# Key stack loads moved ahead of the first mixture; slot numbers three groups ahead instead of two; one-hots made in their own group; shared products read from PSUM

## The chip, the cores and the metric

One core of a Trainium2 chip runs the whole program. The metric is the device time of one launch in microseconds, the median of three runs: 361.41 us before the change (360.48 to 363.17). One more run was profiled; it took 359.17 us, of which 357.1 us are the span that the trace covers. TensorE is called PE here, VectorE DVE, ScalarE ACT, GpSimd POOL and SyncE SP.

## The reference

Two layers work on x (4 x 256 tokens of 128 features, 1,024 tokens in all) and a context of 96 features. Each layer is a cross attention and then a mixture of experts. The change lies in the first layer's mixture, which is this (E = 64 experts, K = 6 per token, at most CAP = 64 tokens per expert, hidden width 88):

```python
scores = softmax(xf @ gate_w.T)
_, idx = top_k(scores + gate_b, K)
weights = take_along_axis(scores, idx, axis=1)
# tokens of one expert get the positions 0, 1, ... in order; position >= 64 is dropped
xb[expert, pos] = xf[token]
h  = silu(xb @ w1) * (xb @ w3)
yb = h @ w2
y  = zeros.at[token].add(yb[expert, pos] * weight)
z  = silu(xf @ ws1.T) * (xf @ ws3.T) @ ws2.T     # the shared expert, width 176
return y + z
```

The second layer's attention (16 heads of 8 features) follows. It needs its keys in a stacked form, `ks`, which is made of three bf16 parts of the keys. The second mixture (8 experts, 2 per token, width 512) comes last.

## The kernel before

Every engine has its own instruction list, written out by hand; counting semaphores order them, and an engine stops at its first unmet wait. The first mixture works through the 64 experts in 8 groups of 8 (`GE`, `NG`); a group has 8 x 64 = 512 slots, held as 4 pairs of experts with 128 slots each (`NPAIR`). For one group g the steps are:

- `dispatch(g)` (DVE, L1388) compares each token's rank with the slot indices and writes a bf16 0/1 matrix of 4,096 columns into `pbuf`; there are two such buffers.
- `slot_numbers(g)` (PE, L941) multiplies it by the scores and token numbers: 32 matmuls of 10 columns into bank 2.
- `slot_values(g)` (DVE, L1402) reads bank 2 into a slot's weight `wslot`, its token number `token_f` and the integer `slot_token`. Before, these have three buffers.
- Gather (POOL, L507): four indirect DMAs fetch 128 rows of 512 B each from `normalised` in DRAM into `xg`, which has two buffers; gather g waits until `gathered_transposes(g-2)` has read its buffer.
- `gathered_transposes(g)` (PE, L916; transposes at L921) and a copy by ACT (`gathered`, L647) turn the rows into `ctxT`.
- `hidden(g)` (PE, L953), Silu (ACT, L672), product (DVE, L1451), `hidden_transposes(g)` (PE, L966), copy `gT` (ACT, L677), `outputs(g)` (PE): the expert network. The end of `outputs(g)` raises `e_Y`.
- `yh` (ACT, L683) and `yl` (DVE, L1463) split the output in two fp32r parts.
- `slot_onehots(g)` (DVE, L1415; three of the four pairs) and `last_onehot(g)` (ACT, L653; the fourth pair) compare the token numbers with all 1,024 tokens. There are two buffers, in `splits` and in `frbuf`.
- `combine(g)` (PE, L924): 16 matmuls of 512 columns add the group's outputs to their tokens. It runs in the next group, behind `hidden(g+1)` and `slot_numbers`.

The DRAM copy of the normalised rows is stored by ACT (L577), in two halves. SP loads the group weights into a ring of three (`group_weights`, L328; 704 KB and 352 KB); the load for g waits for the outputs of g-3. Behind each of the loads for groups 3 to 6, SP issues two `keys_stacked(i)` (L360), eight in all. Each moves 256 KB from the DRAM scratch `k_parts` to eight partitions of `ks`, one contiguous 32 KB run per partition; rows 8i to 8i+7 for load i. `ks` is first read by the second attention, at 172.1 us in the profile. Everything that SP issues goes through one DMA queue (q1 in the profile); the gathers of POOL go through q0.

The shared expert is computed beside this: `shared_hidden(i)` (PE, L878; two matmuls of 88 x 512 into two banks), `shared_activation(i)` (ACT, Silu of the one and copy of the other), `shared_product(i)` (DVE), for i = 0 to 3, and `shared_outputs` (PE) in group 0, behind `hidden(0)` and `slot_numbers(2)`. `mm` at L772 is the helper through which all matmuls go.

## Time and profile before

| | |
|---|---|
| median of 3 runs | 361.41 us (360.48 to 363.17) |
| profiled execution | 359.17 us, span 357.1 us |
| PE busy | 295.2 us, 83% of the span |
| DVE, ACT, POOL busy | 245.0, 193.0, 139.0 us |
| first mixture, group 0's gather issue to the last `outputs` | 55.2 to 153.1 us |
| share of the chain that ended last | PE 54%, DVE 16%, DMA 11%, of which the gathers 8% |
| DMA | 23.96 MB, 67 GB/s over the span; 130 to 178 GB/s between 80 and 143 us |

Times in the trace count from the start of the span. A window row gives the length of a stretch, the busy time of each engine in it with the number of its instructions, then the granted TensorE clock (1.00 is 2.4 GHz, 0.50 is 1.2 GHz), the mean busy share of the 16 DMA engines and their rate. A DMA packet is counted whole where it starts, so that a long packet shows as a share above 1.00 and then as an empty stretch. In the table of waits a row says how long an engine stood idle before a line, and what ended it. In a row of the timeline the bracket gives the idle time before the instruction and what ended it.

### The profile page before, as it was taken

To read this page: it belongs to the slowest core of one execution; us is meant where nothing else is said; L and a number is where in the kernel's file an instruction comes from. 1 tells how busy PE (TensorE), PEld (TensorE's weight loads), DVE (VectorE), ACT (ScalarE), POOL (GpSimd) and SP (SyncE) were. 2 spreads that over 40 slices of the span, in tenths; PEclk is the share of its full clock that TensorE was granted. 3 is DMA by queue.
4 is the path that set the end of the run, shared out by engine and by line. 5 is a ranking of instruction groups with operands and counts; after the bars stand their busy time and mean duration, and the time that the engine had idled before them with its cause. 6 is when DMAs were issued, how large, how long until landed. Compare 5 with 4: busy or idle time off the path is not lost.

```text
span 357.1 us, 5713 instructions
## 1 busy us (share of the span) xinstructions
PE 295.2 (83%) x2004; PEld 197.3 (55%) x2004; DVE 245.0 (69%) x578; ACT 193.0 (54%) x355; POOL 139.0 (39%) x148
## 2 busy tenths in 40 slices
PE   1996871599777597875489999999898999999995
PEld 0675531458665486662125455554566777777773
DVE  3567799256744523546697787763879988898877
ACT  1355160314344034423227776876696888888881
POOL 5963557464635629274044201010104543254000
PEclk9998795559998879998558999999999999999998
DMA  7923101636899787103405100030000301000001
GB/s 214 281 66 118 30 0 24 38 25 157 155 129 178 162 157 178 61 0 77 87 23 124 23 4 1 3 122 1 0 2 0 105 15 59 0 3 0 0 2 60
DMA packets 12377, 23.96 MB, mean 67 GB/s; under 512 B 2020, under 2 KB 7036, under 8 KB 12029
## 3 DMA queue, kind: packets, MB, share of 16 engines
q1 hardware_dynamic: 10043, 20.39, 22.8%
q0 software_dynamic: 1024, 2.10, 5.8%
q10 hardware_dynamic: 1282, 1.12, 1.1%
q8 instruction: 16, 0.26, 0.3%
q14 instruction: 12, 0.10, 0.1%
HBM read 20.88 MB, written 2.62 MB: 66 GB/s over the span
## 4 chain that ended last, share of the span: by engine, by line
PE 54%; DVE 16%; DMA 11%; ACT 7%; POOL 6%; issue 5%; ACTq 0%; SPq 0%; DVEq 0%; POOLq 0%
PE bank L772 50%; DMA xg<-normalised,slot_token 8%; POOL xg L507 4%; DVE score L1604 2%; DMA packc<-in_packc 2%; DMA big<-q_parts 1%; POOL big L517 1%; DVE pbuf L1393 1%; ACT xnT L658 1%; PE bank L921 1%; DVE xn L1271 1%; POOL rstd L458 1%; PE bank L1102 1%; ACT frbuf L762 1%; ACT pbuf L766 1%
## 5 line engine op out<-in xcount | busy, mean ns | idle before, releaser
L772 PE MATMUL bank<-frbuf,splits 128*128 128x512 f32 x384 | 95.6, 399 | 1.3 <-DVE frbuf L1650 1.0
L772 PEld LDWEIGHTS bank<-frbuf,splits 128*128 128x128 f32 x384 | 69.7, 188 | 21.3 <-issue 5.3
L1650 DVE TENSOR_TENSOR frbuf<-pbuf,frbuf 128x512 fp32r<-128x512 f32 x64 | 53.0, 837 | 11.3 <-ACT pbuf L766 10.5
L507 POOL DMA_INDIRECT xg<-normalised,slot_token x32 | 43.5, 1358 | 41.4 <-DVE slot_token L1413 33.8
L1604 DVE TENSOR_REDUCE score<-bank 128x2 f32<-128x512 f32 x64 | 42.1, 687 | 14.6 <-PE bank L772 13.8
L762 ACT ACTIVATE frbuf<-bank,biases 128x512 fp32r<-128x512 f32 x64 | 44.2, 691 | 13.0 <-PE bank L772 9.6
L738 ACT ACTIVATE pbuf<-bank 128x512 f32<-128x512 f32 x64 | 37.1, 598 | 15.9 <-PE bank L772 15.6
L766 ACT ACTIVATE pbuf<-bank,biases 128x512 f32<-128x512 f32 x64 | 43.8, 684 | 0.0
L772 PE MATMUL bank<-ks,big 128*128 128x256 bf16 x128 | 29.4, 322 | 6.5 <-DVE score L1604 3.7
L552 POOL CAST splits<-ew 128x512 fp32r<-128x512 f32 x16 | 12.7, 796 | 45.6 <-PE bank L772 45.6
L1463 DVE TENSOR_TENSOR frbuf<-bank,frbuf 128x512 fp32r<-128x512 f32 x8 | 5.5, 692 | 33.2 <-ACT frbuf L683 33.2
L677 ACT COPY gT<-bank 88x512 f32<-88x512 f32 x8 | 4.7, 582 | 39.4 <-PE bank L969 39.4
L772 PE MATMUL bank<-big,ks 128*128 128x256 bf16 x128 | 25.2, 285 | 0.4 <-ACT pbuf L738 0.4
L458 POOL TENSOR_TENSOR rstd<-veps,mhalf 128x4 f32<-128x4 f32 (+1 forms) x10 | 9.4, 941 | 37.8 <-DVE veps L1263 35.5
L772 PEld LDWEIGHTS bank<-ks,big 128*128 128x128 bf16 x128 | 9.9, 105 | 25.4 <-DVE score L1604 13.6
L553 POOL TENSOR_TENSOR splits<-ew,splits 128x512 fp32r<-128x512 f32 x16 | 22.3, 1391 | 1.3
L921 PE MATMUL bank<-ident,xg 128*128 128x128 f32 x32 | 6.4, 336 | 18.9 <-DMA xg<-normalised,slot_token 18.9
L772 PE MATMUL bank<-pbuf,vaug 128*9 128x256 f32 x256 | 19.7, 381 | 0.0
L537 POOL CAST nmp<-score 128x16 bf16<-128x16 f32 x8 | 1.6, 198 | 44.5 <-DVE score L1604 44.5
L1393 DVE TENSOR_TENSOR pbuf<-rk,iota_s 128x4096 bf16<-128x4096 bf16 (+1 forms) x10 | 18.5, 1863 | 0.1
L772 PE MATMUL bank<-frbuf 128*128 128x512 f32 (+1 forms) x80 | 16.7, 357 | 1.9 <-ACT frbuf L683 1.9
L651 ACT COPY ctxT<-bank 128x512 f32<-128x512 f32 x8 | 4.7, 585 | 24.5 <-PE bank L921 24.5
(195 smaller groups left out, 529.5 us busy)
## 6 DMA issues: line engine op xcount, KB each, us to landing
big<-in_w SPq DMA_DIRECT2D x8, 704.0 KB
ew<-in_ew SPq DMA_DIRECT2D x16, 256.0 KB, 3.1
big<-in_w SPq DMA_DIRECT2D x8, 352.0 KB
ks<-k_parts SPq DMA_DIRECT2D x8, 256.0 KB
big<-q_parts SPq DMA_DIRECT2D x8, 192.0 KB
k_parts<-parts SPq DMA_DIRECT2D x1, 768.0 KB, 3.9
x<-in_x SPq DMA_DIRECT2D x2, 256.0 KB, 5.5
normalised<-xn ACTq DMA_DIRECT2D x2, 256.0 KB, 2.3
```

The costliest lines, as they stand in the source:

```text
L458: pool.tensor_tensor(out=rstd[:, cs], in0=veps[:, cs], in1=mhalf[:, 0:n], op=ALU.pow).then_inc(ln_rstd, 1)
L507: pool.indirect_dma_start(out=xg[:, g % 2, j, :], out_offset=None, in_=xn_dram, in_offset=bass.IndirectOffsetOnAxis(ap=slot_token[:, g % 3 ...
L552: chained(pool.tensor_copy(high[:, e % 2, :], ew[:, e % RING1, i, :]))
L553: pool.tensor_tensor(out=low[:, e % 2, :], in0=ew[:, e % RING1, i, :], in1=high[:, e % 2, :].bitcast(F32), op=ALU.subtract).then_inc(split, 1)
L738: a.activation(prob1[:, e % NPROB, :], bank[2 + e % 2][:, :], ACT.Exp).then_inc(a_exp, 1)
L762: a.activation(acth[:, n % NA, :], bank[n % 3][:, :], ACT.Gelu, bias=bias).then_inc(f_hi, 1)
L766: a.activation(act[:, n % 4, :], bank[n % 3][:, :], ACT.Gelu, bias=bias).then_inc(f_act, 1)
L772: return pe.matmul(out_, lhsT, rhs, start=start, stop=stop, skip_group_check=True)
L921: ins = pe.transpose(bank[3][:, chunk(j)], xg[:, g % 2, j, :], ident[:, :])
L1393: v.tensor_tensor(out=view(onehots[g % 2][:, c * GS:c * GS + 1], (CAP0, n * GE), (2, CAP0 // 2), (1, 2)), in0=view(rk[:, g, c, 0, 0:1], (2 ...
L1604: v.tensor_reduce(nm1[:, c, 2 * hp:2 * hp + 2], bank[m % 2][:, :].rearrange("p (h k) -> p h k", h=2), X, ALU.max, negate=True).then_inc(a_ ...
L1650: v.tensor_tensor(out=actl[:, n % NA, :], in0=act[:, n % 4, :], in1=acth[:, n % NA, :].bitcast(F32), op=ALU.subtract).then_inc(f_lo, 1)
```

## The change

The change has four parts. SP issues all eight `keys_stacked` loads in one go, as soon as the normalised rows are stored (`xn_out` is 32) and before the loads of groups 3 to 7. PE computes `slot_numbers` three groups ahead, with `wslot`, `token_f` and `slot_token` in four buffers. The one-hots of group g are made in group g itself, on DVE behind the product of group g and on ACT behind its Silu, no longer one group earlier. The shared product reads its second factor from PSUM, so ACT's copies go away; in exchange `shared_hidden(2)` and `(3)` wait for DVE's products 0 and 1, and PE now runs them behind `slot_numbers(0)`.

The diff, without hunks in which only `g % 3` becomes `g % NS`:

```diff
--- before.py
+++ after.py
@@ -181,9 +181,10 @@
 
         xb = ctxT[:, :].rearrange("p (a s) -> p a s", a=2)
         PTs = [splits[:, :, :], frbuf[:, 1024:1024 + NPAIR * T].rearrange("p (j t) -> p j t", j=NPAIR)]
-        wslot = sb("wslot", [P, 3, NPAIR])
-        slot_token = sb("slot_token", [P, 3, NPAIR], U32)
-        token_f = sb("token_f", [P, 3, NPAIR])
+        NS = 4
+        wslot = sb("wslot", [P, NS, NPAIR])
+        slot_token = sb("slot_token", [P, NS, NPAIR], U32)
+        token_f = sb("token_f", [P, NS, NPAIR])
         token_i = sb("token_i", [P, NC, 2], I32)
         xg = sb("xg", [P, 2, NPAIR, P])
         sil, gv = sb("sil", [P, NPAIR, I0]), sb("gv", [P, NPAIR, I0])
...
@@ -362,13 +363,14 @@
                              kscratch[PARTS_K[i]].rearrange("(d h) t -> d h t", d=HD)
                              ).then_inc(ks_in, 16)
 
+            sp.wait_ge(xn_out, 32)
+            for i in range(NCOMB):
+                keys_stacked(i)
+
             for g in range(RING0, NG):
 
                 sp.wait_ge(e_Y, g - RING0 + 1)
                 group_weights(g)
-                if g < RING0 + NCOMB // 2:
-                    keys_stacked(2 * (g - RING0))
-                    keys_stacked(2 * (g - RING0) + 1)
 
             sp.wait_ge(sh_sb, 4)
             for e in range(2):
...
@@ -625,9 +627,8 @@
                     norm_transposed(2)
             def shared_activation(i):
                 a.wait_ge(sh_ps, i + 1)
-                a.activation(shared_silu(i), bank[SH_BANKS[i][0]][0:I0, :], ACT.Silu)
-                a.copy(hs[i // 2][:, half(i % 2)], bank[SH_BANKS[i][1]][0:I0, :]
-                       ).then_inc(sh_sil, 1)
+                a.activation(shared_silu(i), bank[SH_BANKS[i][0]][0:I0, :], ACT.Silu
+                             ).then_inc(sh_sil, 1)
 
             a.wait_ge(c_all, 1)
             a.copy(vaug[:, :, :, HD:HD + 1],
...
@@ -663,7 +664,6 @@
 
             gathered(0)
             a.wait_ge(c_iota, 1)
-            last_onehot(0)
             for g in range(NG):
                 for p2 in range(2):
                     a.wait_ge(e_H, 2 * g + p2 + 1)
...
@@ -673,12 +673,12 @@
                                  bank[5 + p2][:, 0:2 * SI].rearrange(
                                      "p (j i) -> p j i", j=2)[:, :, 0:I0],
                                  ACT.Silu).then_inc(e_sil, 1)
+                last_onehot(g)
                 a.wait_ge(e_gTp, g + 1)
                 a.copy(gT[:, :, :], bank[4][0:I0, :].rearrange(
                     "p (j s) -> p j s", j=NPAIR)).then_inc(e_gT, 1)
                 if g + 1 < NG:
                     gathered(g + 1)
-                    last_onehot(g + 1)
                 a.wait_ge(e_Y, g + 1)
                 a.copy(yh, bank[7][:, :].rearrange("p (j d) -> p j d", j=NPAIR)).then_inc(e_yh, 1)
 
...
@@ -903,11 +903,7 @@
             gate_ranks(0)
             pe.wait_ge(x1_sb, NC)
             shared_hidden(1)
-            pe.wait_ge(sh_sil, 1)
-            shared_hidden(2)
             gate_ranks(1)
-            pe.wait_ge(sh_sil, 2)
-            shared_hidden(3)
 
 
             def onehot(g, c, j):
...
@@ -982,18 +978,21 @@
 
             pe.wait_ge(g_parts, 2)
             slot_numbers(0)
+            for i in (2, 3):
+                pe.wait_ge(sh_sb, i - 1)
+                shared_hidden(i)
             slot_numbers(1)
-            pe.wait_ge(sh_sil, 4)
             gathered_transposes(0)
+            slot_numbers(2)
+            pe.wait_ge(sh_sb, 4)
             for g in range(NG):
                 hidden(g)
-                if g + 2 < NG:
-                    slot_numbers(g + 2)
+                if g + 3 < NG:
+                    slot_numbers(g + 3)
                 if g >= 1:
                     combine(g - 1)
                 else:
                     pe.wait_ge(ld_small, 64)
-                    pe.wait_ge(sh_sb, 4)
                     shared_outputs(0)
                     shared_outputs(1)
                 hidden_transposes(g)
...
@@ -1404,13 +1403,13 @@
                 v.wait_ge(e_W, g + 1)
                 for s in range(2):
                     ps = slice(64 * s, 64 * s + 64)
-                    v.reduce_sum(wslot[ps, g % 3, :],
+                    v.reduce_sum(wslot[ps, g % NS, :],
                                  view(bank[2][ps, NW * s:NW * s + 1], (2 * NW, NPAIR), (1, 3)), X)
                     ins = v.reduce_sum(
-                        token_f[ps, g % 3, :],
+                        token_f[ps, g % NS, :],
                         view(bank[2][ps, NW * s + 3:NW * s + 4], (2 * NW, NPAIR), (1, 2)), X)
                 chained(ins)
-                v.tensor_copy(slot_token[:, g % 3, :], token_f[:, g % 3, :]).then_inc(e_id, 1)
+                v.tensor_copy(slot_token[:, g % NS, :], token_f[:, g % NS, :]).then_inc(e_id, 1)
 
             def slot_onehots(g):
 
...
@@ -1418,28 +1417,27 @@
                 if g >= 2:
                     v.wait_ge(e_comb, g - 1)
                 for j in range(NPAIR - 1):
-                    ins = v.tensor_scalar(PTs[g % 2][:, j, :], iota_t, token_f[:, g % 3, j:j + 1],
+                    ins = v.tensor_scalar(PTs[g % 2][:, j, :], iota_t, token_f[:, g % NS, j:j + 1],
                                           None, ALU.is_equal)
                 ins.then_inc(e_PTv, 1)
 
             def shared_product(i):
 
-                part = hs[i // 2][:, half(i % 2)]
                 v.wait_ge(sh_sil, i + 1)
-                v.tensor_tensor(out=part, in0=part, in1=shared_silu(i),
-                                op=ALU.mult).then_inc(sh_sb, 1)
+                v.tensor_tensor(out=hs[i // 2][:, half(i % 2)], in0=bank[SH_BANKS[i][1]][0:I0, :],
+                                in1=shared_silu(i), op=ALU.mult).then_inc(sh_sb, 1)
 
             dispatch(0, range(4, 8))
             dispatch(1, range(0, 4))
             slot_values(0)
+            for i in range(4):
+                shared_product(i)
             dispatch(1, range(4, 8))
-            shared_product(0)
             slot_values(1)
             dispatch(2)
-            for i in range(1, 4):
-                shared_product(i)
+            slot_values(2)
+            dispatch(3)
             v.wait_ge(c_iota, 1)
-            slot_onehots(0)
             for g in range(NG):
                 v.wait_ge(e_id, g + 1)
 
...
@@ -1449,15 +1447,14 @@
                 for j in range(NPAIR):
                     at = (j % 2) * SI + I0
                     ins = v.scalar_tensor_tensor(out=gv[:, j, :], in0=bank[5 + j // 2][:, at:at + I0],
-                                                 scalar=wslot[:, g % 3, j:j + 1], in1=sil[:, j, :],
+                                                 scalar=wslot[:, g % NS, j:j + 1], in1=sil[:, j, :],
                                                  op0=ALU.mult, op1=ALU.mult)
                 ins.then_inc(e_gv, 1)
-                if g + 2 < NG:
-                    slot_values(g + 2)
                 if g + 3 < NG:
-                    dispatch(g + 3)
-                if g + 1 < NG:
-                    slot_onehots(g + 1)
+                    slot_values(g + 3)
+                slot_onehots(g)
+                if g + 4 < NG:
+                    dispatch(g + 4)
 
                 v.wait_ge(e_yh, g + 1)
                 v.tensor_tensor(out=yl, in0=bank[7][:, :].rearrange("p (j d) -> p j d", j=NPAIR),
```

On PE, ahead of group 0. The rows with `sparts,pbuf` are `slot_numbers` (32 each), those with `xnT,packa 88x512` `shared_hidden` (2 each), `ident,xg` is `gathered_transposes(0)`, `big,ctxT` is `hidden(0)`, and `qbuf,ws` the first of `shared_outputs`. Before:

```order
L772 MATMUL bank<-xnT,packa 88x512 x2
L772 MATMUL bank<-sparts,pbuf 128x10 x64
L921 MATMUL bank<-ident,xg 128x128 x4
L772 MATMUL bank<-big,ctxT 64x176 x8
L772 MATMUL bank<-sparts,pbuf 128x10 x32
L772 MATMUL bank<-qbuf,ws 128x512
```

After the change:

```order
L772 MATMUL bank<-sparts,pbuf 128x10 x32
L772 MATMUL bank<-xnT,packa 88x512 x4
L772 MATMUL bank<-sparts,pbuf 128x10 x32
L917 MATMUL bank<-ident,xg 128x128 x4
L772 MATMUL bank<-sparts,pbuf 128x10 x32
L772 MATMUL bank<-big,ctxT 64x176 x8
L772 MATMUL bank<-sparts,pbuf 128x10 x32
L772 MATMUL bank<-qbuf,ws 128x512
```

`slot_numbers(0)` has moved ahead of two `shared_hidden`, and `slot_numbers(2)` from behind `hidden(0)` to ahead of it.

On SP, from the store of the key parts on. Before:

```order
L357 DMA k_parts<-parts 128x3x1024
L331 DMA big<-in_w 128x1408
L333 DMA big<-in_w 88x1024
L361 DMA ks<-k_parts 8x16384 x2
L331 DMA big<-in_w 128x1408
L333 DMA big<-in_w 88x1024
L361 DMA ks<-k_parts 8x16384 x2
```

After the change:

```order
L358 DMA k_parts<-parts 128x3x1024
L362 DMA ks<-k_parts 8x16384 x8
L332 DMA big<-in_w 128x1408
L334 DMA big<-in_w 88x1024
L332 DMA big<-in_w 128x1408
L334 DMA big<-in_w 88x1024
```

The eight key loads stand together, and the five loads of group weights follow with nothing between them.

On ACT, one group in the middle of the mixture (`ctxT` is the copy of the gathered rows, `xnT` and `frbuf` or `splits` the one-hot, the CAST of `frbuf<-bank` is `yh`). Before:

```order
L677 COPY gT<-bank 88x512
L651 COPY ctxT<-bank 128x512
L658 ACTIVATE xnT<-ew,token_f 128x1024
L661 ACTIVATE frbuf<-xnT 128x1024
L683 CAST frbuf<-bank 128x512
L672 ACTIVATE sil<-bank 128x176 x2
```

After the change:

```order
L672 ACTIVATE sil<-bank 128x176 x2
L659 ACTIVATE xnT<-ew,token_f 128x1024
L662 ACTIVATE frbuf<-xnT 128x1024
L678 COPY gT<-bank 88x512
L652 COPY ctxT<-bank 128x512
L683 CAST frbuf<-bank 128x512
```

The one-hot no longer stands between the copy of the gathered rows and `yh`.

## Rows read from the trace of the kernel before

**Rows 1.** Windows by stage: length, busy PE PEld DVE ACT POOL, clock, DMA, GB/s.
```profile
54.20:65.40 11.20, 1.01 (x32) 0.93 (x32) 8.49 (x15) 0.00 (x0) 8.65 (x6) 0.50 0.19 26
65.40:81.50 16.10, 15.35 (x86) 9.48 (x88) 5.72 (x13) 5.68 (x9) 7.55 (x6) 0.50 0.52 31
81.50:89.50 8.00, 7.76 (x90) 6.49 (x88) 6.33 (x14) 3.34 (x7) 3.94 (x2) 1.00 0.69 171
89.50:101.40 11.90, 8.50 (x92) 6.64 (x90) 6.58 (x15) 4.05 (x8) 8.01 (x7) 1.00 0.87 164
101.40:112.30 10.90, 8.13 (x92) 6.64 (x90) 6.31 (x14) 4.22 (x8) 5.24 (x4) 1.00 0.83 144
112.30:126.60 14.30, 10.58 (x92) 8.49 (x90) 6.42 (x14) 5.09 (x9) 6.20 (x5) 0.74 0.81 152
126.60:136.50 9.90, 9.10 (x92) 7.14 (x90) 4.36 (x13) 3.40 (x7) 4.29 (x5) 0.87 0.97 200
136.50:144.90 8.40, 7.01 (x60) 5.73 (x58) 3.58 (x7) 4.30 (x8) 8.34 (x2) 1.00 0.42 108
144.90:153.10 8.20, 6.63 (x54) 5.14 (x50) 3.23 (x7) 2.99 (x6) 0.47 (x1) 1.00 0.20 66
```
**Rows 2.** Waits of PE, 40 to 155 us: us in total, times, longest.
```profile
PE bank L921 <- DMA xg<-normalised,slot_token: 18.9, 5, 9.0
PE bank L772 <- ACT frbuf L683: 3.1, 4, 1.2
```
**Rows 3.** The chain that ended last, 52 to 160 us: start, us, what.
```profile
60.70 4.64 DMA xg<-normalised,slot_token
...
100.35 10.24 DMA xg<-normalised,slot_token
...
122.74 12.07 DMA xg<-normalised,slot_token
```
**Rows 4.** DMA answer for 86.3 to 86.95 us: packets, MB, share of 16 engines.
```profile
q1 hardware_dynamic: 27, 0.29, 317.2%
```
**Rows 5.** DMA answer for 86.95 to 89.1 us.
```profile
DMA packets 0, 0.00 MB, mean 0 GB/s; under 512 B 0, under 2 KB 0, under 8 KB 0
```
**Rows 6.** DMA answer for 89.75 to 91.8 us.
```profile
q1 hardware_dynamic: 16, 0.26, 101.1%
q0 software_dynamic: 15, 0.03, 22.8%
```
**Rows 7.** DMA answer for 93.25 to 99.3 us, the queue of SP.
```profile
q1 hardware_dynamic: 222, 1.00, 60.8%
```
**Rows 8.** The page's part 6: issues, KB each, us from issue to landing.
```profile
normalised<-xn ACTq DMA_DIRECT2D x2, 256.0 KB, 2.3
```
**Rows 9.** Timeline, stores and loads: start, us, engine, line, operation.
```profile
39.62 0.39 ACTq L577 DMA_DIRECT2D normalised<-xn  x1
...
81.54 0.34 SPq L331 DMA_DIRECT2D big<-in_w  x1
```
**Rows 10.** Window behind the weight load's issue at 81.54 us.
```profile
82.50:82.75 0.25, 0.25 (x8) 0.10 (x5) 0.00 (x0) 0.25 (x2) 0.00 (x0) 1.00 1.79 248
```
**Rows 11.** Timeline, the steps ahead of group 0 and in it.
```profile
37.43 3.44 PE L772 MATMUL bank<-xnT,packa 128*88 128x512 f32 x4
...
54.22 1.22 DVE L1393 TENSOR_TENSOR pbuf<-rk,iota_s 128x2048 bf16<-128x2048 bf16 x1
...
55.35 0.68 DVE L1429 TENSOR_TENSOR qbuf<-qbuf,ew 88x512 f32<-88x512 f32 x1
...
65.47 1.09 PE L921 MATMUL bank<-ident,xg 128*128 128x128 f32 x4 [8.96 <-DMA xg<-normalised,slot_token]
...
67.24 2.62 PE L772 MATMUL bank<-big,ctxT 128*64 128x176 f32 x16 [0.68 <-ACT ctxT L651]
...
69.79 1.02 PE L772 MATMUL bank<-sparts,pbuf 128*128 128x10 bf16 x32
...
71.80 2.29 DVE L1393 TENSOR_TENSOR pbuf<-rk,iota_s 128x4096 bf16<-128x4096 bf16 x1
```

More of the change, by code:

```diff
@@ L509, in _ @@
                         in_offset=bass.IndirectOffsetOnAxis(
-                            ap=slot_token[:, g % 3, j:j + 1], axis=0)).then_inc(e_xg[g], 16)
+                            ap=slot_token[:, g % NS, j:j + 1], axis=0)).then_inc(e_xg[g], 16)
             ones_pair = 0x3F803F80
@@ L657, in last_onehot @@
                     a.wait_ge(e_comb, g - 1)
-                a.activation(xnT[:, :], iota_t, ACT.Abs, bias=token_f[:, g % 3, 3:4], scale=-1.0
+                a.activation(xnT[:, :], iota_t, ACT.Abs, bias=token_f[:, g % NS, 3:4], scale=-1.0
                              ).then_inc(a_step, 1)
```

## The prediction

> **What bounds the kernel now.** I read the windows by stage first [rows 1]. They cut the first mixture at the ends of `outputs(g)`: group 0 ends at 81.5 us, group 7 at 153.1 us. From 81.5 us on PE is the engine with the most work, but only group 1 (81.5 to 89.5) runs without a hole: 8.0 us, PE busy for 7.76. Groups 2 to 5 do the same work and take 11.9, 10.9, 14.3 and 9.9 us. Groups 6 and 7 have no `slot_numbers` left and take 8.4 and 8.2. Ahead of all this PE is nearly idle from 54.2 to 65.4 us, and its granted clock is 0.50, that is 1.2 GHz, until 81.5.
>
> The table of waits names the holes [rows 2]: `gathered_transposes` waits five times for the gather, 18.9 us in all. The longest, 9.0 us, is gather 0, so 9.9 us belong to four later groups. Four more waits, 3.1 us together and at most 1.2, are `combine` waiting for `yh` from ACT. The chain shows how late a gather lands behind its last issue [rows 3]: 4.64 us in group 0, 10.24 and 12.07 us later.
>
> The DMA answers say what those gathers stand behind. Where the two key loads of group 0 begin, 27 packets take 317% of 16 engines for 0.65 us, 33.0 us of packet time [rows 4]; 0.26 of the 0.29 MB are one key load, eight packets of 32 KB. If the 19 small ones took 2.4 us together, a key packet took 3.8. Then no packet at all starts for 2.1 us [rows 5], though gathers have been issued. The second key load is 16 packets (eight are data), 101.1% of 16 engines over 2.05 us, 33.2 us or 4.1 us for each large one [rows 6]. So a key load of 256 KB keeps eight DMA engines for 4 us, and the next follows on the same eight. The next group's weights, 1.00 MB, move only behind it [rows 7]. The key loads are what makes the gathers late.
>
> **The change, part by part.**
>
> *Key loads out of the mixture, and the slot numbers three groups ahead.* Gather g+3 now starts when its buffer comes free, behind `gathered_transposes(g+1)`, at the end of group g. It is needed two groups later, about 16 us; before, it also had to wait for the slot numbers made in the middle of the group, which left a group and a half, some 12 us. With 0.5 MB less per group ahead of it, it should be in time. I take all four waits as gone.
>
> *One-hots in their own group.* ACT's two passes leave the stretch between the copy of the gathered rows and `yh`. They now stand behind Silu, where ACT is idle during `combine` (it is busy 3.3 of 8.0 us [rows 1]); DVE's three are hidden in the same way, as it is busy 6.33 of 8.0. If that cover were gone, the 3.1 us of waits for `yh` would come back.
>
> *The pace after.* Four groups with `slot_numbers` at 8.0 us, three without. For these, 8.4 less 1.2 is 7.2 and 8.2 less the mean wait of 0.8 is 7.4; I take 7.3. That is 32.0 + 21.9 = 53.9 us in the place of 71.6 [rows 1, 2]: a gain of **17.7 us**. It is made of 9.9 of gather waits, 3.1 of waits for `yh`, 1.0 for a `slot_numbers` that moves ahead, and 3.7 mostly for the half clock of groups 4 and 5 (0.74 and 0.87). Next late in this stage is nothing but PE.
>
> *The key loads' new place.* The second half of the rows is stored at 39.62 us and lands 2.3 us later, at 41.9 [rows 8, 9]. A load's first packets start about 1.0 us behind its issue [rows 9, 10], so the train begins near 43.0. SP has nothing else to do until 81.5. But the last issue of gather 0 is at 60.70 us [rows 3], in the middle of the train, and its packets go to the same engines. Eight loads at 3.97 us (the mean of 3.8 and 4.1) are 31.8 us, to 74.8. The lower bound is no hindrance at all. The upper is what the mixture's worst period leaves: 14.3 us less the weights' own 3.7 us (60.8% of 6.05 us [rows 7]), halved, is 5.3 us per load, 42.4 in all. I take the middle, since it is the duration of these very packets with only gathers beside them. The trace speaks for a wait to the end of the train: gather packets issued during the first key load had to let the second go first [rows 5, 6]. One more microsecond, an estimate from the crowding of 1.1 us per gather packet there, and `gathered_transposes(0)` starts at 76, not at 65.47 [rows 11].
>
> The Trainium skill says otherwise (DMA: Bandwidth & Descriptors, "Queues, rings and completion order"): an engine goes round its queues in turn, packet by packet, so each of the four gather packets on it would wait for one key packet only. By that the sum would be some 4 us better, as rival 2 works out.
>
> *Group 0 itself.* From those transposes to the end of `outputs(0)` it was 81.5 - 65.47 = 16.0 us at half clock. `slot_numbers(2)` now stands ahead of `hidden(0)`: transposes 1.09 + 1.02 against a start 1.77 us behind before, 0.4 more. `slot_numbers(3)` then waits for DVE, 0.6 for the values and 2.29 for `dispatch(3)`, instead of following `hidden(0)` after 2.55: 0.5 more [rows 11]. So 16.9 us: group 0 ends at 92.9, **11.4 us later**.
>
> *The shared expert.* The two `shared_hidden` that move behind `slot_numbers(0)` cost 3.44 us each at half clock [rows 11], from 55 (a product of 0.68 us behind 54.22) to 62; then Silu 0.6 and product 0.7, with DVE waiting, then the second half of `dispatch(1)` 1.22, then `slot_numbers(1)` 1.0: PE is ready for the transposes at 65.6. Under a gather that lands at 76 this costs nothing. If the gather is early it is next. The copies that ACT loses (four) lie beside other work: nothing. A product from PSUM I price like one from SBUF, 0.68 us.
>
> *The tail.* POOL clears `big` behind the last `outputs`, as before; its long memset of `ks` follows gather 7 and ends before that. The rest of the program moves as a block.
>
> **Sum.** 17.7 - 11.4 = 6.3 us. The span goes from 357.1 to 350.8 us, the profiled execution from 359.17 to 352.9. The median of the three runs is 2.2 us above the profiled one; I add that: **355.1 us**.
>
> **Rivals.**
>
> 1. *Forecast*, 355.1, its own range 352 to 358 (a key load of 3.5 to 4.3 us). Chance 0.42.
> 2. *Turn by turn.* Gather packets slip in between key packets. The train's gaps lie at 43.0 + 3.97k: 58.9, 62.9, 66.8 and 70.8 us, so the fourth gather packet is through at about 72, and group 0 ends at 88.9: 4 us better than the forecast, 351. For it: nothing forbids it once both queues are deep. Against: [rows 5, 6]. Chance 0.20.
> 3. *No collision* (the loads run faster alone, or gathers pass). Then the shared expert's path decides: transposes at 65.6; `slot_numbers(2)` needs values and `dispatch(2)`, to 68.5, and ends at 69.6; `hidden(0)` starts 2.4 us later than before, plus the 0.5: 17.7 - 2.9 = 14.8, so 346.6. Against: 4 us per load is measured. Chance 0.12.
> 4. *Same within measurement.* The train is as forecast, but gathers in the mixture are still late for half of their 9.9 us, since each still shares its engines with 1 MB of weights: 6.3 - 5.0 = 1.3, so 360. Chance 0.16.
> 5. *Slower.* The train itself stretches, because gathers 0 and 1 take turns in it while it still holds their last packets. Gain and loss are equal where the transposes start at 82.3, that is at 4.8 us per key load. At the upper bound of 5.3 the train ends at 85.4, group 0 at 103.3, and 21.8 - 17.7 = 4.1 us are lost: 365.5. For it: the periods of 11 to 14 us with two such loads in each. Against: 3.8 and 4.1 where they run alone, as for their first 14 us. Chance 0.10. The Trainium skill (SBUF — State Buffer, "Door 1: The DMA port swizzle") counts eight neighbouring partitions as 2 of 16 ports, which by its 436 GB/s is an estimate of 4.8 us per load; the measured 4.0 is used.
>
> **Chances and range.** A median of three runs here cannot tell less than 1%, 3.6 us, from no change. Faster by more than that: rivals 2 and 3 and nearly all of the forecast, 0.68, with a small part of it taken off for steps that I do not see. Within 1%: 0.20. Slower: 0.12. The range of 347 to 361.5 us leaves out the slow rival, the upper edge of the fourth and a part of the third.
>
> **What would show it.** *The train*: the key loads' packets from 43 us on, the DMA share below full but without end until about 75. *The collision*: `gathered_transposes(0)` waiting for its gather to 76 us; a start near 66 with no such wait is rival 3. *The shared expert*: PE busy between 55 and 62 us at clock 0.50. *The pace*: windows of 8.0 and 7.3 us behind group 0, clock 1.00, no wait of L917 for a DMA, no wait of `combine` for `yh`. A wait there of some microseconds is rival 4. The prediction is wrong if group 0 ends before 87 or after 98 us, or if the seven groups behind it take more than 57 us.

## The result

The changed kernel takes **367.01 us** (median of 4 runs, 366.04 to 369.78), the kernel before 360.95 us in the same session; the ratio is 1.018 (95% interval 1.009 to 1.027). It is slower, by 0.9 to 2.7%; 355.1 us and "faster" were forecast. The profiled execution took 366.04 us against 359.17 before, and the forecast's own sum said 352.9 for it: 13.1 us too little. Executions of one and the same kernel differ here mostly by up to 3%, so every ratio compares fast executions only, while the profiled execution of ones_early, behind_gather0 and padded_onehots_first was a slow one.

### The profile page after: what moved, and what is told of

It is laid out like the page before. It is cut to its first block, busy times and chain, and to the rows that moved or that the text cites. A ratio compares the mean times of both kernels' runs of the same rounds, so it can differ in the third digit from the quotient of the medians.

```text
span 364.0 us, 5706 instructions
## 1 busy us (share of the span) xinstructions
PE 296.2 (81%) x2004; PEld 197.4 (54%) x2004; DVE 250.4 (69%) x578; ACT 192.5 (53%) x351; POOL 133.3 (37%) x148
## 4 chain that ended last, share of the span: by engine, by line
PE 59%; DVE 17%; DMA 9%; ACT 6%; issue 4%; POOL 3%; another core or an unknown queue 1%; ACTq 0%; SPq 0%; DVEq 0%; POOLq 0%
PE bank L772 55%; DMA xg<-normalised,slot_token 6%; DVE frbuf L1420 2%; DVE score L1601 2%; DVE pbuf L1392 2%; DMA packc<-in_packc 2%; DMA big<-q_parts 1%; POOL big L519 1%; POOL xg L509 1%; PE bank L965 1%; ACT gT L678 1%; POOL rstd L460 1%; PE bank L801 1%; PE bank L1101 1%
## 5 line engine op out<-in xcount | busy, mean ns | idle before, releaser
L1647 DVE TENSOR_TENSOR frbuf<-pbuf,frbuf 128x512 fp32r<-128x512 f32 x64 | 52.5, 830 | 11.9 <-ACT pbuf L766 11.5
L509 POOL DMA_INDIRECT xg<-normalised,slot_token x32 | 37.3, 1167 | 48.4 <-DVE slot_token L1412 20.9
L554 POOL CAST splits<-ew 128x512 fp32r<-128x512 f32 x16 | 13.1, 820 | 45.8 <-PE bank L772 45.8
L555 POOL TENSOR_TENSOR splits<-ew,splits 128x512 fp32r<-128x512 f32 x16 | 21.9, 1371 | 1.3
L772 PE MATMUL bank<-frbuf 128*128 128x512 f32 (+1 forms) x80 | 18.0, 378 | 4.8 <-DVE frbuf L1420 4.0
L772 PE MATMUL bank<-xnT,packa 128*88 128x512 f32 (+2 forms) x28 | 17.3, 750 | 3.0 <-DVE qbuf L1427 1.5
L1406 DVE TENSOR_REDUCE wslot<-bank 64x4 f32<-64x12 f32 x16 | 2.7, 168 | 23.7 <-PE bank L772 17.5
L917 PE MATMUL bank<-ident,xg 128*128 128x128 f32 x32 | 5.8, 312 | 15.8 <-DMA xg<-normalised,slot_token 15.8
L772 PEld LDWEIGHTS bank<-frbuf 128*128 128x128 f32 x80 | 14.0, 203 | 7.6 <-DVE frbuf L1420 4.3
```

Of the source, the lines that this page charges most:

```text
L509: pool.indirect_dma_start(out=xg[:, g % 2, j, :], out_offset=None, in_=xn_dram, in_offset=bass.IndirectOffsetOnAxis(ap=slot_token[:, g % N ...
L554: chained(pool.tensor_copy(high[:, e % 2, :], ew[:, e % RING1, i, :]))
L555: pool.tensor_tensor(out=low[:, e % 2, :], in0=ew[:, e % RING1, i, :], in1=high[:, e % 2, :].bitcast(F32), op=ALU.subtract).then_inc(split, 1)
L772: return pe.matmul(out_, lhsT, rhs, start=start, stop=stop, skip_group_check=True)
L1647: v.tensor_tensor(out=actl[:, n % NA, :], in0=act[:, n % 4, :], in1=acth[:, n % NA, :].bitcast(F32), op=ALU.subtract).then_inc(f_lo, 1)
```

## The profile after

The windows by stage, cut where each group's `outputs` ends (length, busy PE, PEld, DVE, ACT, POOL, clock, DMA share, GB/s), answer to [rows 1]. The first stretch is the wait for gather 0, then come groups 0 to 7:

```profile
55.30:80.80 25.50, 6.43 (x40) 2.60 (x40) 6.64 (x11) 1.19 (x2) 9.65 (x8) 0.63 0.60 68
80.80:97.40 16.60, 16.09 (x118) 10.46 (x120) 8.74 (x19) 4.48 (x7) 6.60 (x5) 0.50 0.25 18
97.40:107.20 9.80, 8.39 (x92) 6.45 (x90) 6.49 (x14) 4.38 (x7) 3.37 (x4) 1.00 0.66 138
107.20:115.30 8.10, 7.87 (x92) 6.60 (x90) 4.13 (x13) 4.39 (x7) 4.19 (x5) 1.00 0.86 166
115.30:124.60 9.30, 7.86 (x92) 6.55 (x89) 8.35 (x16) 4.27 (x7) 5.31 (x5) 1.00 0.64 148
124.60:132.70 8.10, 7.87 (x94) 6.63 (x92) 4.74 (x14) 4.39 (x7) 4.69 (x5) 1.00 0.83 168
132.70:139.90 7.20, 6.96 (x58) 5.73 (x56) 5.18 (x8) 4.39 (x7) 6.25 (x5) 1.00 0.77 158
139.90:152.80 12.90, 8.64 (x60) 6.92 (x58) 8.81 (x9) 4.38 (x7) 6.88 (x2) 0.87 0.38 98
152.80:160.10 7.30, 6.63 (x54) 5.10 (x48) 3.64 (x8) 3.91 (x6) 0.00 (x0) 1.00 0.20 67
```

Group 0 ends at 97.4 us where it ended at 81.5, and the seven groups behind it take 62.7 us where they took 71.6. So 15.9 us are lost ahead of group 1 and 8.9 won behind it: 7.0 of the span's 6.9 (364.0 - 357.1). What follows group 7 takes 204 us in both.

The main waits of PE, 40 to 170 us (us in total, times, longest), answer to [rows 2]:

```profile
PE bank L917 <- DMA xg<-normalised,slot_token: 15.8, 1, 15.8
PE bank L772 <- DVE pbuf L1392: 6.6, 4, 2.5
PE bank L772 <- DVE frbuf L1420: 4.0, 1, 4.0
...
PE bank L772 <- ACT frbuf L683: 0.8, 1, 0.8
```

Of the five waits for a gather one is left. It lasts 15.8 us, where the longest was 9.0 and all five together 18.9. The waits for `yh` (L683) went from 3.1 to 0.8. Those for `dispatch` (`pbuf`) grew from 2.6 to 6.6 us; 1.2 of that lie behind group 0. New is one of 4.0 us for DVE's one-hots (L1420). The chain answers to [rows 3], and the first row of the transposes to 65.47 in [rows 11]:

```profile
60.20 20.61 DMA xg<-normalised,slot_token
...
80.86 1.11 PE bank L917 x4
```

The DMA answers (packets, MB, share of 16 engines) answer to [rows 5, 6]. First 50.45 to 59.30 us, where the train is nearly alone; then 62.9 to 68.1, with all four gathers issued:

```profile
q1 hardware_dynamic: 31, 0.52, 50.7%
q0 software_dynamic: 16, 0.03, 1.9%
...
DMA packets 16, 0.26 MB, mean 50 GB/s; under 512 B 8, under 2 KB 8, under 8 KB 8
q1 hardware_dynamic: 16, 0.26, 43.1%
```

Sixteen large packets filled 0.507 x 16 x 8.85 = 71.8 us of engine time, **4.49 us** for each. In the second stretch only key packets start, and no packet of a gather for 5.2 us.

Last, the timeline around group 6 (start, us, engine, line, operation):

```profile
136.28 8.82 DVE L1420 TENSOR_SCALAR frbuf<-ew,token_f 128x1024 fp32r<-128x1024 f32 x3
...
137.19 7.37 POOL L514 MEMSET ks<- 3x8192 int32 x1
...
137.61 7.49 DVE L1420 TENSOR_SCALAR frbuf<-ew,token_f 128x1024 fp32r<-128x1024 f32 x1
...
145.16 2.07 PE L772 MATMUL bank<-frbuf 128*128 128x512 f32 x4 [4.03 <-DVE frbuf L1420]
```

The row at 137.61 is the last of DVE's three one-hots alone. It starts 0.4 us behind POOL's memset and ends at 145.10, 0.5 us behind the memset's end; undisturbed, three take 2.07 us together (ones_early). PE then works at half clock: 0.53, 0.50 and 0.50 in the three microseconds from 145 us, after it had stood idle since 141.1.

## The experiments

Each is told with the profiled execution's two measures: where group 0 ends, and what the seven groups behind it take (after the change 97.4 and 62.7). Where a letter is given, it is the theory or rival of the expectation above it. Behind group 7 come 204 to 206 us in all but keys_late.

### Undo or do the key loads alone

```diff
-            sp.wait_ge(xn_out, 32)
-            for i in range(NCOMB):
-                keys_stacked(i)
 ...
                 group_weights(g)
+                if g < RING0 + NCOMB // 2:
+                    keys_stacked(2 * (g - RING0))
+                    keys_stacked(2 * (g - RING0) + 1)
```

> The changed kernel with one part undone: the eight key loads are sent behind the weights of groups 3 to 6 again, two at a time, as before the change. Theory A: in the changed kernel the early train of key loads is what costs, because gather 0 stands under it until 80.9 us; without it gathered_transposes(0) starts near 66.5 us (65.47 before, plus the 1 us by which slot_values(0) is later), group 0 ends near 82.5, and the seven groups behind it take 57 to 63 us because the gathers, three groups ahead, can stand under a pair of key loads without being waited for. Last group ends near 142 to 145, time 350 to 354 us. Rival B: the pair of key loads sent behind a group still holds the gather that is needed next, and the seven groups take 70 us as before: time about 360. Rival C: the train is harmless and the loss sits in the three-ahead order itself: group 0 ends at 82.5 but the seven groups take more than 75 us: 366.

Measured: 366.16 us, 1.008 times before (1.004 to 1.013). Group 0 ends at 83.7, as theory A said, but the seven groups take 72.8, as rival B said, though not for its reason. The waits of the engines from 83 to 145 us have no wait of PE for a gather among them:

```profile
PE bank L771 <- issue: 11.9, 15, 3.8
...
PE bank L771 <- ACT gT L677: 1.2, 5, 0.2
...
DVE wslot L1405 <- remote: 1.1, 1, 1.1
```

PE stands 11.9 us in pieces for nothing that the profile shows, and its clock was 0.86 in group 1 and 0.75 in group 5. The expectation of 350 to 354 failed: the key loads' new place is not alone at fault.

The counterpart is the kernel before with the early key loads alone (the same lines, the other way round).

> The kernel before with one part of the change alone: the eight key loads are sent right behind the stored rows, all else is as before. Theory A: the train holds gather 0, gathered_transposes(0) starts near 80 us and group 0 ends near 96 us (14.5 us later than before); the waits for gathers in the groups behind are gone, those for yh stay, so the seven groups take about 71.6 - 17 = 55 to 60 us. Sum: -12 to -16 + 14.5, time 358 to 363 us, no difference that can be measured. Rival B: with only two groups ahead the gather of group 1 stands under the train as well and is waited for again behind group 0: 366 us or more. Rival C: the train shortens nothing behind it (the gathers there were slow for another reason): the seven groups still take 70 us, time 374.

Measured: 367.24 us, ratio 1.013 (1.005 to 1.021). Group 0 ends at 93.8, the seven take 67.3; waits for a gather in them fall from 9.9 to 3.9 us. Theory A's mechanism stands, its pace of 55 to 60 us was at least 7 us too good. This part alone makes the kernel slower; the interval overlaps that of the whole change.

### The memset of the ones

```diff
+                if g == 0:
+                    chained(pool.memset(ks[KROWS:KROWS + 3, :, :].bitcast(I32), ones_pair))
 ...
-            chained(pool.memset(ks[KROWS:KROWS + 3, :, :].bitcast(I32), ones_pair))
```

> The changed kernel with the memset of the three rows of ones in the key stack moved from behind the last gather of group 7 (there it runs 137.2 to 144.6 us) to behind the four gathers of group 0 (it would run from about 60 to 68 us, while VectorE waits for the first gather anyway). Theory A: GpSimd's memset holds VectorE's one-hots of group 5 for its whole length (8.82 us for three instructions that take 2.1), and PE waits 4.03 us for them and then runs 3.4 us at half clock: group 6 falls from 12.9 to 7.3 us, time 366.5 - 5.6 = 361 us. Rival B: the one-hots of group 5 are slow for another reason, or the stretch behind only moves the wait to another place: 365 to 367 us. Rival C: the memset now delays slot_values(1), the gathers of group 1 and what hangs on them, and 3 us or more are given back: 364.

Measured: 358.46 us, ratio 0.979 (0.972 to 0.986); its profiled execution took 360.45. Group 6 in windows, with the columns as above:

```profile
139.60:146.90 7.30, 7.07 (x60) 5.78 (x58) 3.64 (x8) 4.41 (x8) 1.81 (x1) 1.00 0.55 142
```

The seven groups take 57.4. The 5.6 us between 12.9 and 7.3 are the memset: the wait of 4.0 us is gone, and so is the half clock behind it. Over the seven groups it is 62.7 - 57.4 = 5.3, as expected. This kernel is the base of those that follow.

### Where the key loads stand, and what makes them slow

```diff
+            sp.wait_ge(e_xg[NG - 1], 16 * NPAIR)
+            for i in range(NCOMB):
+                keys_stacked(i)
             sp.wait_ge(sh_sb, 4)
```

> The kernel ones_early with the eight key loads moved to behind the last gather (SyncE waits for gather 7 to land, then sends all eight, ahead of the expert weights of the second mixture). No key load stands under any gather. Theory A: gathered_transposes(0) starts near 66, group 0 ends near 83, the seven groups behind take the 57.4 us that they took in ones_early or a little less, so the last group ends near 140; behind it come the same 204.2 us as in ones_early, keys_alone and keys_back: span 344 to 346, time 347 us. The keys would land near 155, ahead of the 167 at which the second attention can start. Rival B: the keys now land after the attention wants them, or the expert weights behind them come late: the stretch behind the last group grows by 5 us or more, 352 or above. Rival C: the seven groups are slow whenever gathers and weights run together (keys_back took 72.7 with no wait for a gather), and 5 us or more come back: 352 to 357.

Measured: 365.99 us, ratio 1.008 (1.004 to 1.013). Rival B. The mixture came near what theory A said: transposes(0) at 65.5, group 7 ends at 143.8 and not at 140, which is still 10 us earlier than in ones_early. But PE then waits, 130 to 220 us:

```profile
PE bank L773 <- DMA big<-q_parts: 17.8, 1, 17.8
```

The loads were issued at 131.6, when gather 7 had landed, and the store and loads of the second attention's queries queued behind it. The train costs what stands behind it, wherever that is.

Next, other partitions:

```diff
-                sp.dma_start(ks[i * HD:(i + 1) * HD, :, :],
+                sp.dma_start(ks[i:i + 8 * HD:8, :, :],
```

> The kernel ones_early with the eight early key loads written to other partitions: load i goes to partitions i, i+8, ..., i+56 and not to 8i to 8i+7 (the key stack's rows are then in the wrong order; everything else is computed as before). Same bytes, same eight pieces of 32 KB, same place. Theory A (the way into eight neighbouring partitions sets the 4.5 us of a piece): the pieces fall to 2.0 to 3 us, the train ends near 60 to 65 us in place of 78.3, gather 0 lands near 62 to 67, transposes(0) near 66 to 68 in place of 80.45: span 345. Rival B (the engine's own pace sets it): pieces stay at 4.4 to 4.5 us, gather at 80, span 358. Rival C: a part of both, pieces near 3.5.

This kernel leaves the key stack's rows in another order. Measured: one run, 346.91 us, span 344.8; transposes(0) at 64.99 after a wait of 0.8, against 80.45 in ones_early. The DMA answer for 47.1 to 52.2 us:

```profile
q1 hardware_dynamic: 32, 0.52, 50.2%
```

0.502 x 16 x 5.1 = 41.0 us for sixteen large packets: **2.56 us** each in place of 4.49. The same bytes in the same pieces, on an equal number of engines, differ only in the partitions that they are written to. Theory A.

Then the size of the pieces:

```diff
-        kscratch = nc.dram_tensor("k_parts", [3, P, T], BF16, kind="Internal").ap()
+        kscratch = nc.dram_tensor("k_parts", [3, P, T + 32], BF16, kind="Internal").ap()[:, :, 0:T]
```

> The kernel ones_early with 32 elements of padding behind each 2 KB row of the key scratch in DRAM, and nothing else changed: a load's source is then 128 rows of 2 KB that don't join, so the pieces are 2 KB and not 32 KB. Same place, same bytes, same eight partitions. Theory A (the gather's packets take turns with the key loads piece by piece, and the wait is the size of a piece): gather 0 passes between 2 KB pieces and lands within 3 to 8 us of its issue, though the train itself still ends at 75 us or later because the way into eight partitions stays narrow; transposes(0) start near 65 to 70 in place of 80.45, last group ends near 139 to 144, span 344 to 348. Rival B (what holds the gather is the share of the DMA engines that the train takes, whatever its pieces): transposes(0) stay near 80, span 358. Rival C: 2 KB pieces are so much slower that the train reaches under the gathers of groups 1 to 4, and the seven groups take 65 us or more: span 352 or above.

Measured: **352.76 us, ratio 0.971 (0.963 to 0.979)**, faster than both kernels; the profiled execution took 348.47, the others 352.40 to 353.32. The interval overlaps that of ones_early, so what the padding alone gives is shown in the traces and not by the times. Transposes(0) start at 72.9, group 0 ends at 84.7 (it ran in part at whole clock, 0.81 in the mean), the seven take 56.4. Answers for 50 to 54 us, and for 62.9 to 67.0:

```profile
q1 hardware_dynamic: 121, 0.23, 53.3%
...
DMA packets 119, 0.23 MB, mean 55 GB/s; under 512 B 8, under 2 KB 8, under 8 KB 119
q1 hardware_dynamic: 119, 0.23, 52.6%
```

The rate, 0.23 MB in 4 us, is that of the large pieces, so pieces of 2 KB don't make the train shorter. The gather still gets no packet in for 4.1 us, but lands some 7.5 us earlier than with 32 KB pieces (72.9 for 80.45 in ones_early, 80.86 after the change).

Group 0 itself took 11.8 us here and 16.3 in ones_early. That is not the padding: one_gather and no_weights run the same group 0 as ones_early, without it, and took 11.7 us at clock 0.80 and 0.81, while no_gathers took 16.7 at 0.50 and gathers_behind_values, with the padding, 16.6 at 0.51. A clock that rises in group 0 is worth near 5 us, and the same instructions ran at either clock. It would account for the profiled 348.47 beside the other three, though no kernel was profiled twice to show it.

Last, the start of the train behind gather 0, with and without the padding:

```diff
-            sp.wait_ge(xn_out, 32)
+            sp.wait_ge(e_xg[0], 16 * NPAIR)
             for i in range(NCOMB):
```

> As keys_padded, with the key loads sent when gather 0 has landed and not when the normalised rows are stored. In keys_padded the gather landed at 72.9 us and PE waited 7.8 us for it. Theory A: gather 0 lands near 62 as before the change, transposes(0) start near 65.5, gathers 1 and 2 have some 15 us to pass between 2 KB pieces and are not waited for; group 0 ends near 81 to 83 (84.7 in keys_padded), seven groups 56 to 58 us, last group ends near 138, span 342 to 345, time 1.5 to 4 us below keys_padded. Less than the 7.8 comes back, since in keys_padded TensorE's clock was whole from 77.5 us and group 0 took 11.8 us behind its transposes, where at half clock it takes 16 to 18. Rival B: the train now lies under gathers 1 to 3 and the weights of group 3 (sent behind it on the same ring, due at hidden(3)), and 5 us or more are lost in groups 1 to 3: 350 or above. Rival C: group 0 runs at half clock to its end and nothing comes back: 346.

Measured: 354.44 us, ratio 0.982 (0.977 to 0.987). Transposes(0) start at 65.4, but group 0 ends only at 88.4, and the seven take 60.8: rival B, and worst in the group that was not named. Rival C has a part in it, since the clock was 0.50 in all 23.0 us of group 0, with PE busy for 16.67 of them. The gathers of groups 1 and 2 are now issued while group 0 computes (timeline):

```profile
71.84 0.16 DVE L1407 TENSOR_REDUCE wslot<-bank 64x4 f32<-64x12 f32 x1 [3.33 <-remote]
...
73.38 2.19 POOL L510 DMA_INDIRECT xg<-normalised,slot_token  x1 [0.30 <-issue]
74.09 0.32 ACT L673 ACTIVATE sil<-bank 128x176 f32<-128x176 f32 x1 [6.95 <-remote]
```

The last matmul of `slot_numbers(2)` ended at 69.6 us and that of `hidden(0)` at 72.1: DVE and ACT got their signals 2.3 and 2.0 us later.

> The same without the padding: eight key loads of 32 KB pieces, sent when gather 0 has landed at about 62 us. Theory A (a gather waits out the train when its pieces are 32 KB): the train runs from 62 to 97; gather 1 (needed at 82) lands near 90 to 98, transposes(1) wait 8 to 15 us, and the weights of group 3 land late too: last group ends near 150 to 155, span 354 to 359. Rival B (a gather that is issued early enough passes even so): 343 to 346, as with the padding.

Measured: 365.34 us, ratio 1.009 (1.004 to 1.013). Theory A: in the profiled execution (369.25 us) the transposes of gather 1 wait 13.8 us and start at 97.6; with the padding they waited 1.6.

### What holds the groups behind

First without the weight loads of groups 3 to 7:

```diff
-                sp.wait_ge(e_Y, g - RING0 + 1)
-                group_weights(g)
 ...
-                pe.wait_ge(ld_w0[g], 32)
+                pe.wait_ge(ld_w0[g % RING0], 32)
```

> The kernel ones_early without the weight loads of groups 3 to 7 (these groups use the weights of groups 0 to 2 again: that part of the computation is left out). What is disputed is why groups 1 to 4 take 10.2, 8.1, 9.3 and 8.0 us where groups 5 to 7 take 7.3: in these PE pauses without waiting for anything shown and slot_values starts up to 2.84 us late. Theory A: the weight loads, 1.06 MB at 300 to 400 GB/s within 6 us of the group's end, hold the engines' semaphores or instructions: without them groups 1 to 4 take 7.5 to 8 us each, seven groups 52 us, span 353. Rival B: the gathers of the group do it, or the semaphore of slot_numbers is late for a reason of PE's own: groups 1 to 4 stay at 8 to 10 us, 57 us, span 358.

Then without their gathers:

```diff
-                for j in range(NPAIR):
+                for j in range(NPAIR if g < 3 else 0):
                     pool.indirect_dma_start(
```

> The kernel ones_early without the gathers of groups 3 to 7 (these groups compute on the rows gathered before: that part is left out). Theory B: the gathers' issue on GpSimd and their small packets are what stops the engines in groups 1 to 4: without them these groups take 7.5 to 8 us each, the seven 52 us, span 353. Rival A (weight loads): they stay at 10.2, 8.1, 9.3, 8.0 and the span at 358. Both may have a part: then the two runs without weights and without gathers each give 1 to 4 us.

Measured, one run each: without the weights 355.14 us, seven groups 56.7 (8.0, 9.5, 9.2, 8.1 us for groups 1 to 4); without the gathers 357.21 us, seven groups **54.2** (8.3, 8.0, 8.1, 8.0). The gathers are the cause of nearly all of it. The other profiles with four gathers agree: the seven groups took 57.4 us in ones_early and 56.4 in keys_padded. The seven groups and one of them, without gathers:

```profile
97.00:151.20 54.20, 52.09 (x516) 42.96 (x512) 34.34 (x79) 30.20 (x48) 1.81 (x1) 1.00 0.43 129
...
113.30:121.40 8.10, 7.87 (x92) 6.59 (x90) 6.41 (x14) 4.41 (x8) 0.00 (x0) 1.00 0.45 136
```

How they do it, two runs asked. The first issues one gather of four:

```diff
-                for j in range(NPAIR):
+                for j in range(NPAIR if g < 3 else 1):
                     pool.indirect_dma_start(
```

> The kernel ones_early with only the first of the four gathers of each group from 3 on (the other rows of these groups are those gathered before: left out). no_gathers took 54.2 us for the seven groups and ones_early 57.4. Theory A (what counts is that gathers are being issued when PE signals the end of slot_numbers, about 1.5 us into the group; one issue of 0.95 us at the group's start is over by then): 54.2 to 54.6, as without gathers. Rival B (in proportion to the number of packets): 55.0.

Measured: 350.99 us, seven groups 54.0. Theory A, though it doesn't exclude an effect of number that sets in above one.

```diff
-                pool.wait_ge(e_id, g + 1)
+                pool.wait_ge(e_id, min(g + 2, NG) if g >= 3 else g + 1)
```

> As keys_padded, but GpSimd issues the gathers of group g (from group 3 on) only when VectorE has finished slot_values(g+1), that is some 2 us into a group and not at its start. Theory A (the issue of gathers holds back what is signalled at that moment): slot_values starts within 1 us of the end of slot_numbers in groups 1 to 4, dispatch is never late, PE's pauses are gone from slot_numbers; the seven groups take 54 to 55.5 us against 56.4, 1 to 2 us better. Rival B (the issue holds whatever runs beside it): PE's pauses move into combine and the one-hots, same time as keys_padded or up to 3 us worse (as padded_onehots_first, 63.2). Rival C: a gather becomes late for its transposes, a wait for it shows: 2 us or more worse.

Measured: 353.51 us, ratio 0.979 (0.970 to 0.988). First a group of ones_early, then one of this kernel:

```profile
107.98 0.96 PE L773 MATMUL bank<-sparts,pbuf 128*128 128x10 bf16 x32
...
110.40 0.95 POOL L510 DMA_INDIRECT xg<-normalised,slot_token  x1 [0.30 <-issue]
...
112.30 0.16 DVE L1407 TENSOR_REDUCE wslot<-bank 64x4 f32<-64x12 f32 x1 [2.84 <-remote]
```

```profile
90.21 0.96 PE L773 MATMUL bank<-sparts,pbuf 128*128 128x10 bf16 x32
...
91.96 0.15 DVE L1407 TENSOR_REDUCE wslot<-bank 64x4 f32<-64x12 f32 x1
...
92.93 1.20 POOL L510 DMA_INDIRECT xg<-normalised,slot_token  x1 [10.84 <-DVE slot_token L1413]
```

`slot_values` starts 3.4 us behind the last matmul of `slot_numbers` when four gathers are being issued, 1 us behind the last issue; with none before it, 0.8 us. That half of theory A holds. Its time doesn't, and the median isn't apart from that of keys_padded: rival C, two later transposes wait 4.6 us for their gathers, the clock is 0.50 from 123.0 to 129.8 us, and the seven groups take 61.1.

The last try at the same loss:

```diff
+                slot_onehots(g)
                 if g + 3 < NG:
                     slot_values(g + 3)
-                slot_onehots(g)
```

> As keys_padded, and VectorE makes the one-hots of a group ahead of slot_values of three groups later, not behind it. In ones_early slot_values started up to 3.2 us late while GpSimd sent the gathers, the one-hots and dispatch stood behind it, and slot_numbers of the next group waited up to 1.2 us on PE; without gathers the seven groups took 54.2 us and not 57.4. Theory A: the one-hots fill that pause, dispatch ends 2 us earlier, and of the 3.2 us 1.5 to 2.5 come back: seven groups 55 to 56 us, time 1.5 to 2.5 us below keys_padded. Rival B: the rest of the loss sits on PE (its own pauses in group 1) and nothing changes: same time as keys_padded within 0.5 us. Rival C: slot_values comes later and with it the gathers, and a wait for a gather shows: 1 us or more slower.

Measured: 356.59 us, ratio 0.971 (0.961 to 0.981), which is not apart from keys_padded: the four executions took 350.15, 353.65, 359.54 and 360.33 us, and whether theory A's 1.5 to 2.5 us are in them can't be told. The profile is that of 359.54 us. In it groups 1 to 4 took 10.2, 10.3, 10.7 and 10.3 us, with PE pausing 12 times for 4.9 us, but none of the quicker ones was profiled, so this isn't shown to be the order's doing.

### The order of the change without its key loads

> The kernel before the change with three things alone: key loads right behind the stored rows, the padding of the scratch rows, and the ones behind the gathers of group 0. Slot numbers and gathers stay two groups ahead, one-hots a group ahead, shared products by way of ScalarE. Theory A: once no key load holds a gather, two groups ahead are enough, and what three ahead and the own group's one-hots bring is only the waits for yh (0.8 to 1.2 us a group, 3 to 4 us): span 347 to 351. Rival B: at two ahead the gathers are waited for in groups 1 to 5 even with nothing else on the rings (they are issued about 6 us before they are needed): 355 or above. Rival C: the order of the change brings nothing at all, 344 to 347.

Measured: 363.17 us, ratio 0.998 (0.988 to 1.007). Group 0 ends at 89.8, the seven take 67.0. Their waits for gathers are 5.3 us and for `yh` 2.0. Rival B. Against keys_padded, with the same key loads and the same memset, the rest of the change (slot numbers three ahead, one-hots in their own group, products from PSUM) is worth 10.4 us, 2.7% by the ratios; the two intervals don't overlap. The three parts of that rest were not measured one by one.

## Why the prediction was wrong

- **The key loads' duration**: "Eight loads at 3.97 us". It is 4.49 where they run without a pause, so the train ended near 79, not 74.8. The 3.8 and 4.1 came from pairs with a pause ahead of each, [rows 4 to 6]; why those were quicker is not shown. What holds the long train is the way into eight neighbouring partitions (keys_spread: 2.56). The Trainium skill (SBUF — State Buffer, "Door 1: The DMA port swizzle") gave the estimate of 4.8 us that was set aside; the measured 4.49 lies nearer to it, and by it the train would have ended at 81.4.
- **The collision**: forecast right in kind, `gathered_transposes(0)` wait for the train's end. Start 80.86, not 76: 4.1 us for the train, the rest for the gather's last turns. The rule of the Trainium skill (DMA: Bandwidth & Descriptors, "Queues, rings and completion order"), by which rival 2 let each gather packet wait for one key packet, has the trace partly on its side: gather packets did come in between, 10 of them (with their signals) beside 4 packets of the key loads' queue from 68.1 to 69.0 us. But on the engines of the train the first turn came 12 us behind the first issue at 56.16 (no gather packet from 62.9 to 68.1 us), and the four turns then reached to the end. Smaller pieces did shorten the turns (keys_padded, 7.5 us), but not that first wait.

```profile
q1 hardware_dynamic: 4, 0.07, 58.9%
q0 software_dynamic: 10, 0.03, 35.7%
```

- **Group 0**: 16.9 us forecast, 16.5 measured. That it would run at half clock was taken over from before and not argued; in other executions the same group took 11.7 (see keys_padded), so the fit is in part luck. The shared expert's two steps at their new place cost nothing, as said: PE was idle under the gather.
- **Waits in the groups**: "I take all four waits as gone" held, and those for `yh` fell to 0.8 of 3.1. That 0.8 belongs to `combine(7)`, behind the last `outputs`, in both kernels; so of the 3.1 us that the forecast named as a part of its 17.7 only 2.3 lay in the seven groups. The 17.7 itself is a difference of paces and doesn't change by it.
- **The pace**: the failed step, "32.0 + 21.9 = 53.9 us". It took 62.7. 5.3 are the memset (ones_early), 3.2 the gathers (no_gathers: 54.2, which is nearly the sum's own figure). The tail's "its long memset of `ks` follows gather 7 and ends before that" priced the memset at its end and not at its neighbour: DVE's one-hots, which now stand in that window. In the kernel before the memset lay from 136.06 to 143.0 us, between two sets of one-hots, and touched the second for 0.1 us only. That set took 3.70 us for 2.1, beside POOL's next memset, of `big`, from 143.06 us on; so the trace of before did show that a memset stretches these instructions:

```profile
136.06 6.94 POOL L512 MEMSET ks<- 3x8192 int32 x1
...
142.88 3.70 DVE L1421 TENSOR_SCALAR frbuf<-ew,token_f 128x1024 fp32r<-128x1024 f32 x3 [2.54 <-PE bank L772]
...
143.06 2.31 POOL L517 MEMSET big<- 64x2048 f32 x1
```

  "Next late in this stage is nothing but PE" overlooked that a signal of PE can be late while gathers are issued, as group g+3's are at each group's start.
- **Sum**: both failed terms count, the train and the pace. 4.5 us ahead of group 1 and 8.8 behind it make 13.3 of 13.1. The slow rival had the right sign and size (365.5) and had the first third of it in a longer train, though not for its reason: it blamed gathers that take turns, and a load took 4.49 us where the train was nearly alone. The transposes started at 80.86, short of its break-even of 82.3, and the pace did the rest.

Left open: by what way four gather issues delay PE's signals and instructions. Their timing is shown, the path is not. Nor is it settled why PE pauses so long in keys_back, or what decides in which executions the clock rises in group 0. Whether the same eight partitions would take a key load faster from all sixteen engines was not measured.

## What to carry to other kernels

A load is priced by what stands behind it on the same engines and by the partitions that it writes to: eight rows of 32 KB into neighbouring partitions hold eight engines for 4.5 us, and a gather behind eight of them came when they ended, in both places where they were put ahead of one (after the change and in behind_gather0). Before counting an engine's moved work as hidden, list what its neighbour runs at that time; a GpSimd memset of 7 us can hold one VectorE instruction of 0.7 us to its end. And a change that loses may hold a good part: here the order was worth 2.7% once the pieces were 2 KB and the memset stood under a wait.

## What was not expected of the hardware

- A memset of 3 x 8192 elements on GpSimd lasts 6.9 to 7.4 us and holds a TENSOR_SCALAR of VectorE until its end (7.49 us for 0.7; the three together 8.82 for 2.1). Beside the same memset in ones_early a CAST of 128x4 took 2.58 us for 0.17, to the memset's end, but a TENSOR_TENSOR of `dispatch` only 2.50, where it takes 2.29 without:

```profile
60.11 6.92 POOL L515 MEMSET ks<- 3x8192 int32 x1
...
64.56 2.50 DVE L1393 TENSOR_TENSOR pbuf<-rk,iota_s 128x4096 bf16<-128x4096 bf16 x1
```

- Eight 32 KB pieces into eight neighbouring partitions: 4.49 us each; into every eighth partition: 2.56 us.
- While four gathers are issued (4 x 0.95 us), the signal of PE's last matmul reached VectorE or ScalarE 2.0, 2.3 and 3.4 us behind it (padded_behind_gather0, ones_early), where it was 0.8 us with no gather being issued (gathers_behind_values), and PE can pause between matmuls that wait for nothing (11.9 us in keys_back).
- The same group 0, behind the same wait, ran in 11.7 us at clock 0.80 (one_gather) and in 16.7 at 0.50 (no_gathers).
